# One-core macaron block: beta from rounded parts, norms from turned k and q, gate statistics in four row groups, new PSUM banks, roots taken early

## The reference, cut to what matters

```python
# x: (8 sequences, 512 tokens, 256 channels), all float32
x = x + 0.5 * ffn(layernorm(x))          # ffn: gelu(x @ w1 + b1) @ w2 + b2, 256 -> 1024 -> 256
x = x + attn(layernorm(x))
x = x + 0.5 * ffn(layernorm(x))

def attn(x):                             # 4 heads of 64
    q, k, v = (silu(causal_conv4(x @ W)) for W in (Wq, Wk, Wv))
    beta = sigmoid(x @ Wb)               # one number per token and head
    q = q * rsqrt(sum(q * q, -1) + 1e-6)
    k = k * rsqrt(sum(k * k, -1) + 1e-6)
    delta = delta_rule(q, k, v * beta, k * beta, chunk=32)   # inverse of a 32x32 triangle per chunk, then a scan
    branches = [fir3(v), fir31(v), delta, v]
    # gate: hidden layer over x, the 4 branches and mean, rms, max of each branch over its 64 channels
    w = softmax(gelu(head_in @ gW1 + gb1) @ gW2 + gb2) ; floor and renormalise
    o = sum(w[i] * branches[i])
    return (o * rsqrt(mean(o * o) + 1e-5) * onorm_w) @ Wo
```

## Time and profile before

| | us |
|---|---|
| median of 3 runs | 1334.34 (1330.45 to 1338.84) |
| the profiled execution's own time | 1321.46 |
| its span | 1319.8 |
| PE busy | 1152.2 (87%), 10204 matmul instructions |
| DVE busy | 806.1 (61%) |
| ACT busy | 547.3 (41%) |
| POOL busy | 395.3 (30%) |
| mean granted TensorE clock | 0.921 of full speed |

### The profile page before, as it was taken

How to read it: one execution, slowest core, us unless ns; L and a number is a source line. 1 busy time by engine, 2 the same in 40 slices (tenths; PEclk the granted TensorE clock), 3 DMA queues, 4 the chain that set the end, 5 groups by cost and what they waited for, 6 DMA issues and landing times.

```text
span 1319.8 us, 25278 instructions
## 1 busy us (share of the span) xinstructions
PE 1152.2 (87%) x10204; PEld 826.6 (63%) x10204; DVE 806.1 (61%) x1542; ACT 547.3 (41%) x965; POOL 395.3 (30%) x637
## 2 busy tenths in 40 slices
PE   3778599899988998889997999889997999887828
PEld 3644485488636884378745885478735885477427
DVE  6753266765766565765776666765775666653253
ACT  1154236443563335443463336533463336531312
POOL 6007300941058100751038200841048100840000
PEclk9988799989998998989998999989997999985758
DMA  5040104010131103010040204010130104010000
GB/s 142 17 91 8 31 17 97 1 31 17 52 62 22 26 17 86 11 31 17 17 96 1 47 17 90 7 31 18 33 81 17 32 1 92 5 31 17 1 0 17
DMA packets 80244, 47.17 MB, mean 36 GB/s; under 512 B 55808, under 2 KB 73728, under 8 KB 80128
## 3 DMA queue, kind: packets, MB, share of 16 engines
q1 hardware_dynamic: 80128, 45.56, 15.2%
HBM read 30.86 MB, written 14.68 MB: 35 GB/s over the span
## 4 chain that ended last, share of the span: by engine, by line
PE 61%; DVE 20%; ACT 8%; issue 4%; POOL 3%; SPq 2%; DMA 1%; DVEq 0%; POOLq 0%; ACTq 0%
PE psum L765 12%; PE psum L766 10%; PE psum L767 10%; DVE conv_acc L1338 6%; PE psum L796 4%; DVE arena L1571 3%; PE psum L1072 3%; PE psum L951 3%; PE psum L936 2%; PE psum L970 2%; PE psum L975 2%; ACT arena L567 2%; SPq L342 2%; DVE arena L1295 2%; DVE arena L1573 1%
## 5 line engine op out<-in xcount | busy, mean ns | idle before, releaser
L512 POOL TENSOR_TENSOR l_prod<-arena 64x30 f32<-64x30 f32 (+14 forms) x240 | 145.0, 604 | 629.4 <-DMA arena<-l_dram 611.2
L563 ACT ACTIVATE h_f<-psum,b_col 128x512 f32<-128x512 f32 x128 | 87.9, 687 | 238.0 <-PE psum L767 231.3
L765 PE MATMUL psum<-w_hi,h_hi 128*128 128x256 f32 x512 | 152.5, 298 | 8.8 <-DVE h_lo L1318 8.7
L516 POOL TENSOR_TENSOR arena<-arena,l_prod 64x30 f32<-64x30 f32 (+14 forms) x240 | 150.8, 628 | 18.8
L767 PE MATMUL psum<-w_hi,h_lo 128*128 128x256 f32 x512 | 144.8, 283 | 0.0
L766 PE MATMUL psum<-w_lo,h_hi 128*128 128x256 f32 x512 | 144.7, 283 | 0.0
L1072 PE MATMUL psum<-v_shift,fir_w 128*32 128x512 f32 x1152 | 142.7, 623 | 0.0
L765 PE MATMUL psum<-xt_hi,w_hi 128*128 128x512 f32 x256 | 116.3, 454 | 22.0 <-DVE xt_lo L1304 13.2
L796 PE MATMUL psum<-ident,arena 128*128 128x128 f32 x384 | 58.7, 309 | 79.9 <-DVE arena L1295 39.7
L1338 DVE SCALAR_TENSOR_TENSOR conv_acc<-psum,conv_col,conv_acc 128x511 f32<-128x511 f32 x144 | 107.8, 749 | 32.3 <-ACT conv_acc L588 21.6
L1317 DVE CAST h_hi<-h_f 128x512 fp32r<-128x512 f32 x128 | 62.0, 484 | 100.0 <-ACT h_f L563 55.2
(11 more groups left out here) (229 smaller groups left out, 2247.9 us busy)
## 6 DMA issues: line engine op xcount, KB each, us to landing
x_in<-in_L_attn_x SPq DMA_DIRECT2D x8, 512.0 KB, 4.0
v_dram<-v_fm SPq DMA_DIRECT2D x8, 512.0 KB, 2.8
v_shift<-v_dram SPq DMA_DIRECT2D x8, 512.0 KB, 5.0
out<-x_tok SPq DMA_DIRECT2D x8, 512.0 KB, 2.9
v_shift<-v_dram SPq DMA_DIRECT2D x8, 511.0 KB, 6.9
v_shift<-v_dram SPq DMA_DIRECT2D x8, 510.0 KB, 9.1
v_shift<-v_dram SPq DMA_DIRECT2D x8, 509.0 KB, 10.9
arena<-in_L_ffn_w SPq DMA_DIRECT2D x2, 1024.0 KB, 7.4
```

What stands on the lines that cost most here:

```text
L512: pool.tensor_tensor(prod, l_inv[:, k + 1:, k:k + 1].broadcast_to(shape), l_inv[:, k:k + 1, 0:k].broadcast_to(shape), ALU.mult).then_inc(i ...
L516: pool.tensor_tensor(l_inv[:, k + 1:, 0:k], l_inv[:, k + 1:, 0:k], prod, ALU.add).then_inc(inverted, 1)
L563: act.activation(h_f[:, m % 2, :], bank, ACT.Gelu, bias=b1_col[:, m:m + 1]).then_inc(read, 1)
L765: pe.matmul(dst, a_hi, b_hi, start=first, stop=False, **kw)
```

## The change

Seven things are done together.

1. **Beta** is taken with `product3` from rounded parts of `Wb` (`wb_hi`, `wb_lo`, made once), six instructions instead of eight, into a bank of its own; ACT's Sigmoid is set between `silu(1)` and `silu(2)`, and `beta_turn` turns it.
2. **Norms of k and q**: the sums with `kq_sel` go. k is turned to tokens first (`k_t`), ACT squares it straight from PSUM, and DVE sums over 64 channels (`tensor_reduce`). For q a turn `q_t` is added that serves the norm alone.
3. **Gate statistics**: `stat` writes four row groups of 32 (sums, sums, maxima, maxima), and each head's product over 64 rows becomes two products over 32 rows, in two rounds over the four heads, with a semaphore (`half_stats`) between the rounds.
4. **PE's order**: k's turn, the k products ("gram"), `q` and `hidden`; `attend(0)` moves from before the FIRs' second half to behind the turn of `ln3`; six FIR slots instead of five stand before `mix_t`; `attend(1)` and `lpair` move later in the last FFN (8 to 16, 18 to 20).
5. **DVE's order**: `q_rows` moves from behind the output norm to ahead of it; `attend(0)` moves into the last FFN; `normalise(0)` and the splits are reordered.
6. **ACT's order**: all four `gate_gelu` before `tap(5)`; both roots before the copies out of `v_t` and `f_t`.
7. **PSUM banks** of the pass are dealt out anew. Setup gets 2 more DVE operations for the rounded `Wb` and 4 for `gate_st`.

```diff
-        K = [("k", (0, 1)), ("rows", (3,)), ("gram", (0, 1)), ("rows_t", (3,)), ("q", (4, 7)), ("k_t", (2, 5)), ("hidden", (3,))]
-        LOGIT = [("logit", (6,)), ("logit_t", (6,))]
-        FIR = [("fir", (0, 1, 2, 5))]
-        Q = [("rows_q", (3,)), ("rows_qt", (6,)), ("at0", (4, 7))]
-        MIX = [("mix_t", (0, 1)), ("wo", (3, 6))]
-        V_T = [("v_t", (0, 1)), ("f_t", (2, 5, 4, 7)), ("lhalf", (0, 1))]
-        FFN_C = [("ln3", (3, 6)), ("upc", (2, 3) * (KT // 2)), ("outc", (5, 6))]
-        L_OFF = [("at1", (4, 7)), ("lpair", (0, 1))]
-        NEXT = [("next", (0, 1))]
+        K = [("k", (0, 1)), ("beta", (4,)), ("q", (3, 5)), ("beta_t", (4,)), ("k_t", (0, 1)), ("gram", (7, 2)), ("hidden", (6,))]
+        LOGIT = [("logit", (4,)), ("logit_t", (4,))]
+        FIR = [("fir", (7, 2, 0, 1))]
+        Q = [("q_t", (3, 5))]
+        MIX = [("mix_t", (6, 4)), ("wo", (7, 2))]
+        V_T = [("v_t", (3, 5)), ("f_t", (0, 1, 6, 4)), ("lhalf", (3, 5)), ("at0", (7, 2))]
+        FFN_C = [("ln3", (6, 4)), ("upc", (0, 4) * (KT // 2)), ("outc", (1, 6))]
+        L_OFF = [("at1", (3, 5)), ("lpair", (7, 2))]
+        NEXT = [("next", (7, 2))]
...
@@ ScalarE, one_pass
                     tap(3)
+                    out_of(at, "beta", 0, beta_fm[:, :], ACT.Sigmoid, src=lambda b: b[0:32, :])
                     silu(2)
                     silu(3)
-                    act.wait_ge(silu_made, 6 * j + 4)
-                    for h in range(HALVES):
-                        act.activation(sq[:, h, :], qk_fm[:, h, 0, :], ACT.Square).then_inc(kq_squared, 1)
-                    rows, read = arrive(act, at, "rows")
-                    act.activation(rows_fm[0:32, :], rows[0:32, :], ACT.Copy)
-                    act.activation(rows_fm[32:64, :], rows[32:64, :], ACT.Sigmoid).then_inc(read, 1)
+                    for t in range(2):
+                        bank, _ = arrive(act, at, "k_t", t)
+                        act.activation(sq[:, t, :], bank, ACT.Square).then_inc(kq_squared, 1)
...
-                    gate_gelu(0)
-                    gate_gelu(1)
+                    for h in range(HEADS):
+                        gate_gelu(h)
                 if at.front:
                     tap(5)
                 if at.back:
-                    gate_gelu(2)
-                    gate_gelu(3)
...
+                    for t in range(2):
+                        bank, read = arrive(act, at, "q_t", t)
+                        act.activation(at_flat[:, 512 * t:512 * t + 512], bank, ACT.Square).then_inc(kq_squared, 1)
...
+                if at.next:
+                    root(0, j + 1)
+                if at.back:
+                    root(2, i)
+                if at.front:
                     for b in range(2):
                         out_of(at, "v_t", b, ...)
                     for t in range(TILES):
                         out_of(at, "f_t", t, ...)
-                if at.next:
-                    root(0, j + 1)
-                if at.back:
-                    root(2, i)
@@ TensorE
+            def gate_stats(at):
+                for s, heads in enumerate(STAT_HEADS):     # ((0, 1, 2, 3), (2, 3, 0, 1))
+                    if s == 1:
+                        pe.wait_ge(half_stats, HEADS * (at.i + 1))
+                        pe.sem_inc(passed, 1)
+                    for g, h in enumerate(heads):
+                        bank, full = where(at, "gate", h)
+                        pe.matmul(bank, gate_st[32 * g:32 * g + 32, s, :], stat_fm[32 * g:32 * g + 32, :],
+                                  start=False, stop=(s == 1)).then_inc(full if s == 1 else half_stats, 1)
...
                     projection(at, "v", 1, 2)
-                    for m in range(2):
-                        projection(at, "k", m, 0)
+                    projection(at, "k", 0, 0)
+                    beta(at)
+                    projection(at, "k", 1, 0)
                 if at.back:
                     pe.wait_ge(stat_made, i + 1)
-                    for h in range(HEADS):
-                        gate_stats(at, h)
-                if at.front:
-                    k_rows(at)
+                    gate_stats(at)
+                if at.front:
+                    projection(at, "q", 0, 1)
+                    beta_turn(at)
+                    pe.wait_ge(silu_made, 6 * j + 4)
+                    to_tok(at, "k_t", lambda h: qk_fm[:, h, 0, :])
+                    k_products(at)
                     projection(at, "q", 1, 1)
-                    to_tok(at, "k_t", lambda h: qk_fm[:, h, 0, :])
...
                     firs(at, 0, range(1, 9))
-                    q_rows(at)
                     pe.wait_ge(silu_made, 6 * j + 6)
-                    attend(at, 0)
-                    q_rows_turn(at)
-                    firs(at, 1, range(0, 5))
+                    to_tok(at, "q_t", lambda h: qk_fm[:, h, 1, :])
+                    firs(at, 1, range(0, 6))
...
-                    firs(at, 1, range(5, 7))
+                    firs(at, 1, range(6, 7))
...
-                attend_at, pair_at, next_at = 8, 18, len(STEPS) - 4
+                attend_at, pair_at, next_at = 16, 20, len(STEPS) - 4
                 if at.back:
                     turn_rows(at, "ln3", xn_made[2], i + 1)
+                if at.front:
+                    attend(at, 0)
@@ VectorE
                 def k_rows():
-                    bank, read = arrive(dve, at, "rows_t")
-                    for r in range(2):
-                        ins = dve.tensor_copy(rows_tok[:, r, :]..., bank...)
-                    link(ins)
+                    bank, read = arrive(dve, at, "beta_t")
+                    link(dve.tensor_copy(rows_tok[:, 1, :]..., bank...))
                     dve.sem_inc(read, 1)
+                    dve.wait_ge(kq_squared, 4 * j + 2)
+                    link(dve.tensor_reduce(rows_tok[:, 0, :], sq_u, AX.X, ALU.add))
...
                 def q_rows():
+                    dve.wait_ge(kq_squared, 4 * j + 4)
+                    link(dve.tensor_reduce(rows_tok[:, 2, :], q_sq, AX.X, ALU.add))
...
+                if at.front:
+                    q_rows()
                 if at.back:
                     dve.wait_ge(mix_squared, i + 1)
                     link(dve.tensor_reduce(oss[:, :], sq_u, AX.X, ALU.add))
...
                 if at.front:
-                    q_rows()
-                    attend(0)
                     q_inverse()
...
                     split(1, i, 1)
+                if at.front:
+                    attend(0)
+                if at.back:
+                    split(1, i, 2)
+                if at.front:
+                    off_diagonal("lhalf")
+                if at.back:
+                    split(1, i, 3)
                 if at.next:
                     normalise(0, j + 1, x_in)
```

More of the change, by code:

```diff
@@ L470, in _ @@
                 make(pool.memset(mean_sel[:, half, part], 1.0 / D))
-                for hh in range(HALVES):
-                    make(pool.memset(kq_sel[part, hh, 2 * hh + half:2 * hh + half + 1], 1.0))
             for par in range(2):
@@ L975, in gate_d, with beta, beta_turn, k_products @@
                 pe.matmul(bank, gate_w[:, 2, :], dv_fm[h], start=False, stop=False)
-            def gate_stats(at, h):
-                bank, full = where(at, "gate", h)
-                pe.matmul(bank, gate_st[:, h, :], stat_fm[0:64, :], start=False, stop=True).then_inc(full, 1)
-            def k_rows(at):
-                j = at.j
-                bank, full = claim(pe, at, "rows")
-                for k in range(HALVES):
-                    for n, part in enumerate((xt_hi, xt_lo)):
-                        pe.matmul(bank[32:64, :], wb_pad[:, k, :], part[:, k, :].bitcast(F32), start=(k + n == 0),
-                                  stop=(k + n == 2))
-                for h in range(HALVES):
-                    pe.wait_ge(kq_squared, 4 * j + h + 1)
-                    last = pe.matmul(bank[0:32, :], kq_sel[:, h, :], sq[:, h, :], start=(h == 0), stop=(h == 1),
-                                     skip_group_check=True)
-                last.then_inc(full, 1)
+            def gate_stats(at):
[7 more added lines that the diff above has]
+                                  start=False, stop=(s == 1)).then_inc(full if s == 1 else half_stats, 1)
+            def beta(at):
+                bank, full = claim(pe, at, "beta")
+                for k in range(HALVES):
+                    last = product3(pe, bank[0:32, :], wb_hi[:, k, :], wb_lo[:, k, :], xt_hi[:, k, :], xt_lo[:, k, :],
+                                    k == 0, k == HALVES - 1)
+                last.then_inc(full, 1)
+            def beta_turn(at):
+                copied(pe, at, "beta")
+                bank, full = claim(pe, at, "beta_t")
+                pe.sem_inc(passed, 1)
+                for t in range(TILES):
+                    last = pe.transpose(bank[:, 32 * t:32 * t + 32], beta_fm[:, P * t:P * t + P], ident[0:32, 0:32])
+                last.then_inc(full, 1)
+            def k_products(at):
```

(31 more changed lines are left out.)

71 lines of the change are left out of this document (36 added, 35 removed).

## The result

The changed kernel takes **1271.26 us** (median of 4 runs, 1264.83 to 1274.17) against 1333.07 (4 runs, 1330.45 to 1338.84): a ratio of 0.956, 95% interval 0.952 to 0.961, or 58.4 us off 1333.07 by the ratio. (The kernel before has one run more here than in the table ahead of the prediction.) The forecast was 1289 (gain 45.3) in a range of 1272 to 1311: the median lies 0.7 us under the range's low end, and by the ratio, taken off the 1334.3 that the forecast started from, the time is 1275.9, inside it. The profiled execution took 1264.83 us with a span of 1263.1; before it was 1321.46 and 1319.8, 56.7 us more.

What follows compares the result with a forecast made beforehand. PE is busy 138.9 of 147.5 us, but the chain of waits leaves it mid-pass. Gains of 6.3 us per pass times 7, plus head 2.5, minus tail 0.9 and setup 0.4, make 45.3 off 1334.3: 1289 us, range 1272 to 1311.

Steps and rivals of the forecast that it cites:

- Convolution stage, cost 0: Between silu(1) and silu(2): beta's sigmoid and two table loads, 3.15 us, fit ACT's holes of 3.24; bounds 0 and +0.6.
- its rival: Each new ACT table load stalls as long again, silu(3) 2.5 us late: 17.5 us back, 1306; chance 0.03.
- 0.1 us to spare: Room left on ACT around beta's sigmoid before silu(3) would start later.
- Norm of k and gelu, 2.0: From k's turn to the mixing's start: earlier norm and gelus gain 2.0 us per pass; bounds 1.0 and 2.2.
- Norm of q, loss 0.6: Between mixing and output norm: q's sum on DVE covers a 1.12 us wait, loses 0.6 per pass; bounds 0.4 and 0.8.
- Roots, 2.4: Before the last FFN: root ahead of six ACT copies lets DVE go on sooner, 2.4 us per pass; bounds 2.0 and 2.6.
- Clock at the last FFN, 2.2: PE's shorter idle before ln3's turn avoids the fall to 0.50: gain 2.2 us per pass; bounds 0 and 2.4.
- inside it, 0: Within the last FFN: moved attend, lhalf, normalise and new bank users counted as neither gain nor loss.
- The 1311 and 1303 rivals: 1311: last FFN still starts at half clock, chance 0.13; 1303: copies hold ln3's turn 2 us, root gains 0.4, 0.07.
- Inversion slack: POOL's inversion: last load lands 12.7 us before the next merge, more than the 6.3 gained, so it does not bound.
- Only one low stretch per pass: Expected sign in PE's clock: full clock in the last FFN's first 5 us, one low stretch left per pass.
- The rival with stalls in every pass: PE stops without a releaser in the k products in all 7 passes, 53 us lost: 1342; chance 0.02.

Runs made afterwards that it cites:

- beta_again: Changed kernel with beta's sigmoid done twice, 0.6 us more of ACT between silu(1) and silu(2): 1275.83 us, ratio 0.963.
- gelu_split: Changed kernel with the old ACT order, two gelus, tap(5), two gelus: 1277.61 us, ratio 0.964.
- q_sum_late: Changed kernel with q_rows() moved back behind the output norm, next to q_inverse(): 1271.97 us, ratio 0.960.
- roots_only: Kernel before the change with only the two roots moved ahead of the copies out of v_t and f_t: 1299.1 us, ratio 0.977.
- pair_bias: Changed kernel with v's shifted loads sent two and two, and the last FFN's bias added by one DVE operation instead of POOL's four: 1265.83 us, ratio 0.954.
- warm_mix: Changed kernel with sixteen unread matmuls ahead of PE's wait before mix_t: 1272.41 us, ratio 0.958.
- paired_warm: Changed kernel with v's shifted loads sent two and two and 120 unread 32x32 matmuls at the head pass's end: 1258.6 us, ratio 0.946.

## Why the prediction was right, and where it was off

- **Convolution stage, cost 0:** held. Both loads and the sigmoid stand back to back (628.76, 630.06, 630.66, 631.96). So the drain of some 1380 ns that the Trainium skill ("ScalarE: Activation LUTs", "What ACT_TABLE_LOAD costs") adds to a load is not seen here either, and its rival is out. The "0.1 us to spare" was too small: beta_again puts 0.6 in without a trace, since DVE's gate sums, not `silu(3)`, hold the norm sum.
- **Norm of k and gelu, 2.0:** measured 2.39 in the pass that was read, 2.05 by the medians. DVE was forecast to start at 667.4 with the copy ahead of the k sum; the sum stands at 636.71 + 31.11 = 667.8. gelu_split gives about 0.6 of the gain to the order of the gelus.
- **Norm of q, loss 0.6:** this step failed, in sign. `lsum` to `oss` became 0.7 shorter. The sum replaced the wait, as said, and q_sum_late shows that it costs nothing there; what had not been counted is that the mixing itself is shorter, 8.22 us for its four operations where it was 8.87. Both run beside POOL's inversion. In the tail, where no inversion runs, the four take 8.20 from the first's start to the last's end in both kernels; beside it they took 8.87 to 9.10 so measured before, and 8.2 to 8.3 in four of the seven passes of the changed kernel. In those they run as if alone, while operations of POOL take some 2.25 each (last section). What decides who waits is not shown.
- **FIR and wo, 0.3:** 0.4. **Roots, 2.4:** 2.55, and 2.47 and 2.56 alone and undone. The copies of that term's rival did vanish from the path: PE waits 0.29 for the turn. **Clock at the last FFN, 2.2, and inside it, 0:** 2.5 from `ln` to the merge, but only 1.4 with the roots alone. The four passes of roots_only that keep 1.00 there are 1.5 to 2.2 shorter than before, and the same passes of the changed kernel another 0.0 to 1.1. So the clock gives most of it, less than forecast in three of the four, and the rest, which the forecast had at 0, makes up the sum; which of the moved steps gives it is not shown. The 1311 and 1303 rivals are out, though one argument against the first misreads its rows: the clock was not at 1.00 for all of the FIRs, since the first sixteen ran in the stretch with a mean of 0.62.
- **Head 2.5:** 2.8. **Tail, loss 0.9:** a gain of 0.7, within its bounds. **Inversion slack:** the last loads are issued by 702.33 + 2.95 = 705.28 and the merge is at 710.08, so some 2.8 us are left of the 12.7 if they land 2 us later, as forecast. Most of what went is the pass's own gain. Beside that, `l_tok` is stored 1.7 us earlier, but its loads follow 3.43 us later instead of 2.04, so the inversion starts when it did (648.93 + 31.11 = 680.04, before 680.1), and it takes 44.8 us where it took 42.3. By the landings in the trace, the seven merges behind the head's had 9.1 to 15.7 us of slack before and have 10.2, 0.4, 1.0, 3.3, 9.4, 2.2 and 0.3 now, the large ones behind the two stopped passes. The inversion is about to bound the pass: with both edits of pair_bias three merges wait 0.7 to 1.6 us for its loads.
- **Only one low stretch per pass:** not quite. The one at `mix_t` stayed in six passes of seven, a short one is new at the norm of k in two passes and before the logits in a third, and the one at the last FFN is gone. warm_mix prices the one at `mix_t` at 0.8 us, and shows no gain in the whole.
- **Stops without a releaser:** two, as before, and they became longer (7.6 and 8.3 us against 3.5 and 5.1). A stopped pass is about 9 us longer than the others: 18 us in the seven, some 10 more than before. In the three passes that stop in neither kernel and do not follow the head (4, 6 and 7) the gain was 8.2, 9.6 and 7.9 us, not 6.3, and the stops gave the difference partly back. The rival with stalls in every pass is out. The 45 of the forecast and the 57 of the spans are closer than the terms deserve: the largest term, the roots, was right, but of the others some were too small and one had the wrong sign.

## What to carry to other kernels

Look first for short instructions that stand behind long ones on their engine while another engine waits for them: two roots moved ahead of six copies were worth half of the whole change. Before pricing work put into an engine's queue, see what that engine waits for right behind it; here a sum that filled a wait was free, and an engine held in its spare time (the cast of 4.22 us) cost nothing either. When a kernel's runs spread by 1%, cut each pass at fixed events: the profiles here differed most in one low-clock stretch after the head and in the number and length of the stops, and the edits of paired_warm shortened both.

## What the runs showed of the hardware that was not expected

- TensorE stopped for 6 to 8 us, with no semaphore involved, while four 0.5 MB loads were out (DMA share 0.98 and 0.84 in the changed kernel's two stops), and for 2 to 5 us with two. Others, of 2 to 6 us, stood before the last merge, with none of these loads out.
- An idle of only 1.29 us on TensorE was followed by a stretch at 0.50 in one pass and, at 1.28 us, by 1.00 in another, both with a DMA share above 1. After the longer wait at the head's end the low stretch lasted anything from some 4.5 to 23.5 us.
- Sixteen fp32 matmul instructions of 32 rows on four row groups took 2.54 us, 0.16 each; the eight of 64 rows before took 0.46 each.
- VectorE and GpSimd held each other up both ways: the cast of 4.22 us above, which took 0.47 with GpSimd's additions gone, and, beside mixing's 4.66 us pair, a small operation of GpSimd that took 2.24 us. The same step of the inversion in the next pass, which ran ahead of the mixing, took 0.30:

```profile
649.95 2.24 POOL L519 TENSOR_TENSOR arena<-arena,l_prod 64x58 f32<-64x58 f32 x1
...
792.81 0.30 POOL L519 TENSOR_TENSOR arena<-arena,l_prod 64x58 f32<-64x58 f32 x1
```
